# A graph layer on one core: edge stage with a third set of gathered rows, node-tile scores written a chunk earlier, and the softmax links between single weighings

## The reference

```python
    feat_v = (feat @ W_val + b_val).reshape(N, HEADS, OUT_FEATS)
    e = el[src] + er[dst]                       # (E, 8)
    e = jnp.where(e >= 0, e, NEG_SLOPE * e)
    e_max = jax.ops.segment_max(e, dst, num_segments=N)
    exp_e = jnp.exp(e - e_max[dst])
    denom = jax.ops.segment_sum(exp_e, dst, num_segments=N)
    a = exp_e / jnp.maximum(denom[dst], 1e-16)
    msg = feat_v[src] * a[:, :, None]
    rst = jax.ops.segment_sum(msg, dst, num_segments=N)
```

## Time and profile before

| | us |
|---|---|
| median of 3 runs | 3391.83 |
| lowest, highest | 3384.01, 3405.29 |
| the profiled execution, its own time | 3404.08 |
| its span in the profile | 3402.2 |

### The profile page before, as it was taken

How to read it: one execution, slowest core, us unless ns; L and a number is a source line. 1 busy time by engine, 2 the same in 40 slices (tenths; PEclk the granted TensorE clock), 3 DMA queues, 4 the chain that set the end, 5 groups by cost and what they waited for, 6 DMA issues and landing times. The chain is left out here.

```text
span 3402.2 us, 50353 instructions
## 1 busy us (share of the span) xinstructions
PE 2323.1 (68%) x11245; PEld 1760.3 (52%) x11246; DVE 1814.0 (53%) x3898; ACT 1045.2 (31%) x2749; POOL 1302.6 (38%) x1406
## 2 busy tenths in 40 slices
PE   4999998565776777777776677776333339999400
PEld 3777776223555555555555455555333328888300
DVE  5444443687666666656655565564444334444433
ACT  0111111002443444444434343443533313333100
POOL 0000000301655555655555555561243352222244
PEclk8999998898888788888888887888555559999755
DMA  3122212644555555655555655663655634444576
GB/s 118 58 70 70 68 64 82 215 167 149 170 159 168 165 165 173 180 175 169 172 161 166 183 170 152 177 185 118 208 130 136 131 72 141 145 146 144 176 251 233
DMA packets 238376, 508.79 MB, mean 150 GB/s; under 512 B 50320, under 2 KB 76432, under 8 KB 238208
## 3 DMA queue, kind: packets, MB, share of 16 engines
q0 software_dynamic: 85936, 274.85, 27.8%
q1 hardware_dynamic: 134752, 196.94, 18.8%
q10 hardware_dynamic: 17520, 35.44, 3.2%
HBM read 394.73 MB, written 112.37 MB: 149 GB/s over the span
## 5 line engine op out<-in xcount | busy, mean ns | idle before, releaser
L637 POOL DMA_INDIRECT arena<-v_table,idx x832 | 879.9, 1058 | 834.2 <-PE ps L1575 575.9
L1575 PE MATMUL ps<-arena 128*128 128x260 f32 x3328 | 948.0, 433 | 0.7 <-DVE arena L1192 0.7
L1575 PEld LDWEIGHTS ps<-arena 128*128 128x128 f32 x3328 | 679.0, 215 | 121.9 <-issue 7.3
L776 ACT ACTIVATE arena<-ps x832 | 502.8, 604 | 442.9 <-issue 359.0
L1397 PE MATMUL ps<-arena 128*128 128x24 bf16 (+4 forms) x1994 | 396.0, 329 | 243.8 <-ACT arena L767 107.5
L1192 DVE TENSOR_TENSOR arena<-arena 128x512 f32<-128x512 f32 x832 | 537.2, 685 | 0.0
L1397 PEld LDWEIGHTS ps<-arena 128*128 128x128 f32 (+1 forms) x1994 | 261.4, 191 | 386.4 <-issue 159.9
L1402 PE MATMUL ps<-ident,arena 128*128 128x128 f32 x1128 | 213.9, 308 | 299.9 <-DVE arena L1270 242.8
L1402 PEld LDWEIGHTS ps<-ident,arena 128*128 128x128 f32 x1128 | 150.9, 160 | 321.9 <-DVE arena L1270 247.7
L767 ACT ACTIVATE arena<-arena 128x24 bf16 x832 | 180.5, 217 | 269.5 <-issue 189.5
L677 POOL DMA_INDIRECT arena<-xn_table,e_idx x105 | 99.3, 946 | 282.1 <-PE ps L1402 264.7
(11 more groups left out here) (263 smaller groups left out, 3584.3 us busy)
## 6 DMA issues: line engine op xcount, KB each, us to landing
y_table<-arena SPq DMA_DIRECT2D x105, 256.0 KB
arena<-local_table ACTq DMA_DIRECT2D x52, 512.0 KB
arena<-in_x SPq DMA_DIRECT2D x98, 256.0 KB
arena<-v_table,idx POOLq DMA_INDIRECT x832
v_table<-arena SPq DMA_DIRECT2D x49, 260.0 KB, 3.0
agg<-arena SPq DMA_DIRECT2D x49, 260.0 KB
arena<-agg SPq DMA_DIRECT2D x49, 260.0 KB
x_mix<-arena SPq DMA_DIRECT2D x49, 256.0 KB
```

The lines of the kernel that those rows point to most:

```text
L637: pool.indirect_dma_start(vg[:, j % 2 * U + i, :], None, v_table, bass.IndirectOffsetOnAxis(ap=idx[:, j, i:i + 1], axis=0))\
L776: act.activation(halves(fin[:, bass.ds(room, DH)], HALF), halves(ps[:, bass.ds(room, 2 * D)], D)[:, :, 0:HALF], ACT.Copy).then_inc(s("act_ ...
L1575: return pe.matmul(sums[h], hot[:, i // V, i % V, :], vg[:, b * U + i, h * HALF:(h + 1) * HALF], start=False, stop=False)
```

## The change

`chunks` is new: four chunks unrolled, a loop of seven laps of six chunks, six unrolled; POOL goes through it as well. Places are taken by k, the chunk's number inside the lap.

- Gathered rows: `vg` has RING = 3 times 16 = 48 places; POOL waits for `step_mm` of three chunks ago; `idx` has six places; a third semaphore `rows_in2`. Some buffers change their place in the arena.
- Tile scores: `er_cur` has two places. In chunk c ACT writes those of chunk c+3 (before: c+2), still after `er_mm` of c+1. At the start it writes three chunks' scores.
- ACT's `factor` stands after the 7th step (was 6th), `weights` and `chunk_in` after the 11th (was 9th). Two loads of words a chunk, one for each chunk's word; before, one load served a pair of chunks.
- PE: `turned_e` goes from after the 2nd step to the chunk's start, ahead of L1600; `spread_ends` from the 6th to the 7th, `turned_max` from the 9th to the 11th; `expanded` stands after the 8th, 12th and 15th (was 7th, 11th, 15th).
- DVE: the blocks are taken apart into single links, one or two between weighings. The first three (`summed_parts`, `both_ends`, `leaked`) stand after the 1st, 2nd and 3rd weighing; they were after the 6th. The last scan stands after the 15th weighing (was 12th), `shifted` after the 16th (was 14th).

The core of the diff:

```diff
-BETWEEN = (6, 10, 14)
+BETWEEN = (7, 11, 14)
+RING, LAP, OPEN_CHUNKS = 3, 6, 4
...
+def chunks(eng, body):
+
+    laps = (NCH - OPEN_CHUNKS) // LAP - 1
+    for k in range(OPEN_CHUNKS):
+        body(0, k)
+    with eng.Fori(0, laps) as i:
+        for j in range(LAP):
+            body(i, OPEN_CHUNKS + j)
+    for k in range(OPEN_CHUNKS + laps * LAP, NCH):
+        body(0, k)
...
-                    if later(c, 2) and i % 2 == 0:
-                        apart(pool, s("step_mm"), c * U + (i + 2 - 2 * U))
+                    if later(c, RING) and i % 2 == 0:
+                        apart(pool, s("step_mm"), c * U + (i + 2 - RING * U))
...
-                (d, word), (d2, word2) = own[0], own[-1]
+                (d, word), = chunk_places(ENGINE.Activation, c, 1)
                 if ahead:
+                    (d2, word2), = chunk_places(ENGINE.Activation, c + 3, 1)
                     act.wait_ge(s("er_mm"), c + 2)
                 for i in range(U):
                     if ahead:
-                        d2 = tile_scores(i, d2, word2)
+                        d2 = tile_scores(i, b, d2, word2)
...
-                    if i == 5:
+                    if i == 6:
                         factor(c + 1)
-                    elif i == 8:
-                        weights(c + 1, 1 - b)
+                    elif i == 10:
+                        weights(c + 1, (k + 1) % RING)
...
-                    if i == 4 and not (isinstance(c, int) and c == NCH - 2):
-                        turned_hot(c + 2, b, r + 1)
-                    elif i == 5:
-                        scored(c + 1, n, q)
-                    elif i == 7:
-                        run_max(c + 1, n)
+                    if i == 0:
+                        summed_parts(c + 1)
+                    elif i == 1:
+                        both_ends(c + 1, v_next, r_next)
+                    elif i == 2:
+                        leaked(c + 1)
+                    elif i == 4:
+                        max_up(c + 1, b)
+                    elif i == 5:
+                        max_down(c + 1, b)
...
+                    elif i == 13:
+                        joined_up(c + 1, b)
+                    elif i == 14:
+                        joined_down(c + 1, b)
+                    elif i == 15:
+                        shifted(c + 1, v_next)
...
+                if more:
+                    turned_e(c + 1)
                 if later(c, 1):
                     pe.wait_ge(s("rescaled"), c)
...
-                    if i == 1:
-                        turned_e(c + 1)
-                    elif i == 3:
+                    if i == 3:
                         gathered_ends(c + 1)
-                    elif i == 5:
+                    elif i == 6:
                         spread_ends(c + 1)
-                    elif i == 8:
+                    elif i == 10:
                         turned_max(c + 1)
```

More of the change, by code:

```diff
@@ L120, in turns, with number, lap_round @@
         body(t, t % u, t // u)
-def chunks(eng, body, places, ahead, left=1):
-    for c in range(2):
-        body(c, c, 0, places(c, ahead + 1))
-    with eng.Fori(1, NCH // 2 - left) as i:
-        own = places(i * 2, ahead + 2)
-        for j in range(2):
-            body(i * 2 + j, j, i, own[j:j + ahead + 1])
-    for c in range(NCH - 2 * left, NCH):
-        body(c, c % 2, c // 2, places(c, ahead + 1))
+def chunks(eng, body):
[7 more added lines that the diff above has]
+        body(0, k)
+def number(i, k):
+    return i * LAP + k
+def lap_round(i, k, n):
+    return i * (LAP // n) + k // n
 def turn_of(word, i):
@@ L777, in snapshot, with chunk @@
                                ACT.Copy).then_inc(s("act_step"), 1)
-            def chunk(c, b, r, own):
+            def chunk(n, k):
+                c, b = number(n, k), (k + 1) % 2
                 more = not (isinstance(c, int) and c == NCH - 1)
-                ahead = not (isinstance(c, int) and c >= NCH - 2)
-                (d, word), (d2, word2) = own[0], own[-1]
+                ahead = not (isinstance(c, int) and c >= NCH - 3)
+                (d, word), = chunk_places(ENGINE.Activation, c, 1)
                 if ahead:
+                    (d2, word2), = chunk_places(ENGINE.Activation, c + 3, 1)
                     act.wait_ge(s("er_mm"), c + 2)
@@ L812, in _ @@
             chunk_in(2, 0)
-            chunks(act, chunk, lambda c, n: chunk_places(ENGINE.Activation, c, n), 2, 2)
+            chunks(act, chunk)
             act.wait_ge(s("step_mm"), ST)
@@ L1199, in found, with step, chunk @@
                                   dst_local[:, bass.ds(t, V)].unsqueeze(2).broadcast_to([P, V, P]), ALU.is_equal)
-            def step(i, b):
-                v = halves(vg[:, b * U + i, :], HALF)
-                weighed(v, v, v[:, :, D // 2:]).then_inc(s("step_pv"), 1)
-            def chunk(c, b, r, own):
+            def step(i, v):
+                row_ = halves(vg[:, v * U + i, :], HALF)
+                weighed(row_, row_, row_[:, :, D // 2:]).then_inc(s("step_pv"), 1)
+            def chunk(n, k):
+                c, v = number(n, k), k % RING
                 more = not (isinstance(c, int) and c == NCH - 1)
-                n, q = 1 - b, (r if b == 0 else r + 1)
+                b, v_next, r_next = (k + 1) % 2, (k + 1) % RING, lap_round(n, k + 1, RING)
                 for i in range(U):
@@ L1212, in chunk @@
                         dve.wait_ge(s("p_exp"), c + 1)
-                    step(i, b)
+                    step(i, v)
+                    if i == 2 and later(c, 1):
+                        factored(c)
                     if i == 3 and later(c, 1):
-                        factored(c)
                         rescaled(c)
@@ L1233, in _ @@
             turned_hot(0, 0, 0)
-            scored(0, 0, 0)
-            run_max(0, 0)
-            linked(0)
-            joined_max(0, 0)
+            summed_parts(0)
+            both_ends(0, 0, 0)
+            leaked(0)
+            max_up(0, 0)
+            max_down(0, 0)
+            outer_ends(0)
+            links_up(0)
+            links_down(0)
+            moved(0)
+            picked_links(0)
+            own_links(0)
+            carried(0)
+            joined_up(0, 0)
+            joined_down(0, 0)
             shifted(0, 0)
             turned_hot(1, 1, 0)
-            chunks(dve, chunk, lambda c, n: (None,) * n, 0)
+            chunks(dve, chunk)
             def weights_lo(c):
@@ L1538, in expanded @@
                     cols = slice(i * 3 * H, (i + 1) * 3 * H)
-                    last = product(spread[:, cols], [(hot_t[:, i * P:(i + 1) * P], er_cur[:, cols])])
+                    last = product(spread[:, cols], [(hot_t[:, i * P:(i + 1) * P], er_cur[:, b, cols])])
                 if g == U // V - 1:
@@ L1630, in _ @@
             for g in range(U // V):
-                expanded(1, g)
+                expanded(1, 1, g)
             empty(True, False).then_inc(s("tile_sum"), 1)
-            chunks(pe, chunk, lambda c, n: chunk_places(ENGINE.PE, c, n), 0)
+            chunks(pe, chunk)
             def logits(t):
```

148 lines of the change are left out of this document (90 added, 58 removed).

## The result

The changed kernel took 3535.1 us (median of 4 runs, 3529.57 to 3543.58) against 3395.73 of the kernel before beside it: ratio 1.0414 [1.0372, 1.0457], slower. The profiled execution took 3529.57, its span in the profile is 3527.4. The forecast was 3320 us and faster. The same kernel, unchanged, took 3207 against 3281 when the pair was measured again on another chip; what makes that difference is most of what follows.

The account below looks back on a forecast made before the run. Waits passing between engines, no engine being full, were taken as the bound. Period 22.0 + 3.0 end + 2.1 closings + 1.0 late releases + 0.4 laps = 28.5 against 30.0; with +5 for the start, 3320 us, range 3190 to 3440.

Parts of the forecast that it names:

- the term for late releases: DVE's "remote" waits before the rescaling, 49.8 us in the kernel before, kept as 1.0 us a chunk.
- (1): Two places for tile scores: takes away PE's 2.5 us a chunk at the chunk's end, except 1.0 of late releases.
- (3): Links laid singly, sum of parts before the rescaling: chunk's end 4.6 us against 1.3, net +3.0 a chunk.
- the 8.0 us beyond the least period: Period 30.0 less least period 22.0: closings 3.3, chunk's end 2.5, turn of scores (L1545) 1.3, the rest spread.
- (2): 48 places for gathered rows: L1140's 136.9 us and L1545's 1.3 a chunk go; POOL's next limit 22.3 a chunk.
- (4): Tile closings: snapshots on time more often, mean wait 1.4 us instead of 2.8; 2.1 a chunk instead of 3.3.
- (5): Laps of six: loop heads on DVE and PE might cost 7 x 3.3 = 23 us, 0.4 a chunk.
- (6): Before the stage: ACT copies a third chunk's scores, +5 us; sixteen more gathers on POOL, 0.
- What would show it: Signs: L1153 waits 3 to 6 us a chunk for PE; PE's largest wait at L1678 or L1620, 3.8 or more.
- B: Rival, slower: later second maximum pass makes PE wait at its turn (L1632), +2.2 a chunk, 3433 us; chance 0.18.
- C: Rival, code loading: DVE, PE and POOL all wait at each lap in series, 3381 us; chance 0.16.
- A: Rival, faster: without long chunk ends PE's clock stays up, 2.4 us a chunk less, 3173 us; chance 0.16.

Follow-up runs that it names:

- undisturbed sitting: Set of runs made together on one chip in which the unmodified kernel before takes near 3290 us; the changed kernel there took 3207.47 us, 0.9766.
- disturbed sitting: Set of runs made together on one chip in which the unmodified kernel before takes near 3395 us; the changed kernel there had ratios 1.0414 and 1.0321.
- the old order: Changed kernel with sum of parts, source's score and leak in one block behind the rescaling again: 3112.29 us (0.9441) undisturbed, 3357.53 us (0.9862) disturbed.
- laps_only: Kernel before with laps of six alone (32 places, one place for tile scores, old order of links), disturbed: 3404.57 us, 1.0018.
- the second sitting: Undisturbed runs with the unchanged pair: kernel before 3280.85 us, changed kernel 3207.47 (0.9766); local-number loads moved early in each: 1.0106 and 0.9729.
- the first of the five: Undisturbed, kernel before 3293.66 us; changed kernel with early loads 3205.75, no loads 3192.15, no gathers after 48 3227.97, old order of links 3112.29.
- singles_late: Changed kernel with links still laid singly, but sum of parts behind the rescaling and PE's turn of scores later, disturbed: 3341.86 us, 0.984.

## Why the prediction was wrong

The step that failed is the term for late releases: in part (1), "except the 1.0 of late releases, which I keep", and in the sum "+ 1.0 (late releases)". The prediction had seen DVE wait 7.60 us for a release given 6.8 earlier, and took the share of such waits in the kernel before, 49.8 us of "remote" before the rescaling, as a constant. It is none. In the kernel before the late release is `acc_shut`: the trace records it 1.2 us after its giver on the mean (40 ends of the 51 are recorded), and `er_mm`, which is waited for behind the rescaling, only 0.4 after the small products (38 ends). Part (3) put the wait for `er_mm` in front of the rescaling. There it cost 516.2 us of "remote" at L1153, and `er_mm` came 5.6 us after its giver; `acc_shut` came 3.5 late. So two things happened: a second wait came onto PE's path, and the releases themselves came later than before. Had both kept their old lateness, the term would have been 1 to 2 us a chunk; the runs showed 5.5 to 6.1 us a period in all in place of the 1.0. Why they came later is not explained.

In an undisturbed sitting, where late releases are 0, the same working without that term gives 27.5 against 25.9 measured. That the ratio there, 0.977, is what the forecast had (3320 against 3392 is 0.979) is in part luck, since the kernel before also lost its late releases.

The sum has a slip as well: the 8.0 us beyond the least period were told as 7.1 and "0.9 is spread", but the new sum starts from 22.0 and leaves these 0.9 out. With them it gives 29.4 and about 3366 us, inside the stated range and still far from 3535.

Point by point:
- **(1) Scores.** PE's wait for ACT's scores went (106.6 to 1.1). Worth alone, with the laps, 0.2 us a period in the disturbed sitting (29.65 against 29.85) where 2.5 - 1.0 = 1.5 were expected. The end fell by 1.1 (3.20 against 4.26), and the rest of the chunk took 0.9 more: PE's waits went over to L1610 and L1666, as shown above, and DVE waited longer for rows (180.3 against 132.0 us).
- **(2) Places.** The wait of 136.9 went to 0; 1.05 a period alone (28.80 against 29.85), expected 1.3. Right. POOL still waits for PE (600.0 us of it), so its 22.3 did not bind.
- **(3) Links.** Expected +3.0 a chunk net of late releases. Undisturbed, the end is 4.27 against 1.86 in the old order, +2.4, and the period +2.1. The mechanism was right and its size nearly so; what was wrong is the release at its head, taken as "0.1". It was 0.03 in the undisturbed timeline and 6.9 in the disturbed one.
- **(4) Closings.** The waits for snapshots are 74.3 us in the stage, expected 48 x 1.4 = 67. Right.
- **(5) Laps.** Expected 0.4 a chunk; measured alone 1.0018 of the time. Nothing to measure. The Trainium skill (Runtime: NRT & Kernel Launch, "Instruction fetch mechanics") has a fetch at a taken branch that leaves the pages held; the trace has 103 packets on the instruction queue q8 where there were 22, and no wait at PE or DVE that comes every six chunks. So the trace shows more fetching, and no cost of it.
- **(6) Start.** The scores +4.6 (855.5 against 850.9 in laps_only), expected 5. The 16 gathers, costed at 0, were +18.4 (869.3): 16 at 1.25 us are 20. Who waits for them before the stage was not followed.
- **What would show it.** "A new large one at L1153 for PE, 3 to 6 us a chunk" was 10.4 and named "remote"; the largest wait of PE is at L1620, as said, but 8.6 with L1678's and not 3.8.
- **Rivals.** B, the side on which the result fell, was not its cause: L1632 waits 7.6 us in all, 0.15 a chunk, where B needed 1.4. C is excluded by laps_only. A did not come with this kernel where it was forecast (clock 0.80 in the stage, 0.84 before). The clock did rise with the old order in an undisturbed sitting. Windows of the kernel before in the second sitting and of the old order in the first of the five:

```profile
820.00:2225.00 1405.00, 1113.00 (x4936) 805.43 (x4936) 937.60 (x2133) 619.21 (x1706) 849.72 (x849) 0.86 0.62 182
```

```profile
820.00:2040.00 1220.00, 1028.26 (x4976) 753.78 (x4977) 949.43 (x2160) 627.24 (x1726) 855.74 (x832) 0.93 0.71 208
```

The matmuls of nearly the whole stage (4976 against 4936) take 85 us less of PE, at a clock of 0.93 instead of 0.86: 1.7 of the 4.1 us that the period lost there.

The range's upper end was 3440 because B set it; no case had a wait whose length, and not only its existence, depended on its place. Rows 4 and 6 held the warning: a release 6.8 us late at the head of the very stretch that the change moved a second wait into. They did not hold its size.

## What to carry to other kernels

A release that the trace shows late ("remote", though its giver has ended) is not a constant of the kernel: its cost in one order says nothing sure of its cost in another (0.4 us for `er_mm` before, 5.6 after). Before moving a wait onto the path, ask what the forecast would be if that release came as late as the worst one seen, give that case a chance, and prefer an order in which work that needs only an older release comes first. Here the orders with the sum of parts behind the rescaling are faster by about 3% (undisturbed, 0.944 against 0.977) to 5% (disturbed, 0.984 against 1.032). And before experimenting on a loss, run the unchanged kernel again beside the edits: the first of the five sittings told nothing of the cause, because the disturbance was not there.

## What the runs showed of the hardware

- The kernel before takes about 3290 us in some sittings and 3395 in others, on the same chip too. In the second kind, DVE gets PE's release `er_mm` 5.6 us late on the mean in the changed kernel, against 0.01 in the first kind.
- That lateness needs POOL's indexed gathers: none without them (3219.19), none with plain DMAs of the same bytes (3220.09), nearly all of it (5.2 us) with half the bytes (3505.88).
- In the changed kernel's first trace the release, counted from the end of the last weighed product, is the later the more gathers POOL starts between that product's start and it: 1.2 us with none (3 ends), 6.2 with four (8 ends), 9.1 with seven (17 ends). A longer wait also leaves room for more gathers, so this shows nothing by itself; in the undisturbed trace 43 of 50 ends have one gather in this stretch and a release at 0.56.
- ACT gets the same release as late as DVE (L778 at 1600.88). Its "issue" idle before L787 is longer too: 345.3 us with up to 7.5 at once, against 188.4 and 0.6.

Open: what makes a sitting one or the other; whether the indexed descriptors, the length of the gather instruction or the pauses between gathers do it; whether the product or its release is late; why the lateness itself is greater in the changed kernel (`er_mm` 5.6 us and `acc_shut` 3.5 after their givers) than in the one before (0.4 and 1.2); where the old order loses the rest of its 4.6 us; and `singles_late` in an undisturbed sitting, which was not run.
